# Attention on one Trainium2 core: P.V and row sum groups in two halves of 256 queries

## The chip, the cores and the metric

The kernel runs on one core of a Trainium2 chip. The metric is the device time of one execution in microseconds. Engines are named as in the profile: PE is TensorE, DVE is VectorE, ACT is ScalarE, POOL is GpSimd, SP is the engine that issues most loads and stores.

## The reference

The input is 8 batches of 2048 tokens with 256 features. A routed feed-forward block, self-attention and the same feed-forward block follow one another, each with a residual. The change touches attention alone, which is computed after the projections q, k, v for 8 heads of 32 features:

```python
scores = jnp.einsum('bqhd,bkhd->bhqk', q, k) / DH ** 0.5
attn = jax.nn.softmax(scores, axis=-1)
out = jnp.einsum('bhqk,bkhd->bqhd', attn, v)
```

## The kernel before, in words

The whole program is a row of phases, each with a barrier behind it: a scoring pass, the choice of tokens, the routed feed-forward block, the projections, attention (`attend`), and again scoring, choice and feed-forward. Everything is in fp32; scores use the fp32r form.

`attend` cuts the work into 64 units: 8 batches, 2 groups of four heads, 4 slices of 512 queries. A unit runs over 16 chunks of 128 keys, in 16 cycles. For one chunk and one head, a score tile is keys by queries, 128x512, in one of two PSUM banks (`ps_s`); ACT takes the exponential of each tile into `probs`, a ring of 8 chunks. There is no running maximum: the maximum of each query is computed a unit ahead by a second set of score matmuls (`ps_max`, queries by keys) which DVE reduces, and it enters the scores as an additional row of the operands. The order on each engine is written out by hand; semaphores join the engines.

A cycle `i` of a unit on PE, in the loop over `NCYC`:

- `score(j)` and `score(j + 1)`, heads 0 and 1 of chunk `i`. Each is one matmul (L1653) and waits until ACT has read the tile before the last (`exp_done`).
- `pv` of the chunk before (L1617): four matmuls, one for each head, each into its own 32 rows of `ps_acc`, 512 columns wide. fp32 makes each two passes, so the trace has eight records. For chunks 13 and 15 four more with a matrix of ones (L1625) add the same probabilities to the row sum in `ps_misc`. The last matmul increments `pv_done`.
- `score(j + 2)` and `score(j + 3)`, heads 2 and 3.
- `max_four` (L1584): four matmuls of 32 rows each, one per head, into the four banks of `ps_max`. They wait until DVE has reduced the four before.

Some cycles hold more. In cycle 0 the P.V group is that of chunk 15 of the unit before, and ACT copies the finished accumulator behind it (`copy_acc`, L1543). In cycle 3 `close_z` (L1633) adds POOL's part of the row sum, and ACT copies that (`copy_z`). In cycle 4 and cycle 6 four transposes each turn the row sum and the output (L1640, L1647). In cycle 13 the second score is put off: a transposition of the maxima (L1590) takes its bank, ACT copies it out, and then the score runs.

POOL sums the probabilities of the other chunks, so that PE need not (L1437, eight additions a unit, 128x2048 each). For five pairs of chunks a DMA adds the first into the second (L1414, 1 MB each); it is issued by POOL and waits until `pv_done` says that PE has read the second chunk of the pair. ACT may overwrite a chunk of the ring when PE, POOL and the DMA are done with it. The additions are issued in program order on POOL's queue, the waits for the pairs among them. `close_z` waits for the last addition.

Between the first score of a cycle and the last two, the order of the waits on PE is what sets its schedule:

```python
if i > 0:
    pv(unit, un, i - 1)
elif carry:
    pv(unit - 1, (un - 1) % BU, NC - 1)
...
for n in range(2, PER_CYC):
    pe.wait_ge(exp_done, unit * TILES + j + n - 1)
    score(j + n)
...
max_four(i)
```

`carry` is true for all units but the first.

## Time and profile before

| | us |
|---|---|
| median of 3 runs | 4966.07 |
| lowest, highest | 4965.32, 4968.26 |
| the profiled execution, its own time | 4967.85 |
| its span in the trace | 4965.8 |
| PE busy | 3964.8 |
| DVE busy | 3282.3 |
| ACT busy | 2837.2 |
| POOL busy | 2799.9 |

The span is the time from the first to the last record of the trace; the device time is a little longer. Busy times are unions of records. Four P.V matmuls run side by side in four column strips, so their records overlap, and the busy time of the group is far below the sum of the records. "PEld" are the weight loads of PE. In the timelines, records of one kind that follow one another are merged into one row ("x8"), with the time from the first start to the last end; in square brackets stands the idle time of the engine before the row, and what ended it.

### The profile page before, as it was taken

The page shows a single profiled execution, that of the slowest core. Times are in us where ns is not written, and L with a number is a line of the kernel's source. Part 1 is how long each engine was busy: PE and PEld are TensorE (multiplying, and loading weights), DVE is VectorE, ACT ScalarE, POOL GpSimd, SP SyncE. Part 2 cuts the span into 40 slices and gives each one's busy share as a digit, 9 for nine tenths or more (in the row PEclk, how much of TensorE's full clock was granted, in tenths as well). Part 3 has the DMA queues.
Part 4 walks back from the last instruction along what each step waited for, and adds up shares of the span by engine and source line. Part 5 has one row for each costly group of instructions (what it writes and reads, how often), then busy time and mean ns, then how long its engine had stood idle before and what let it go on. Part 6 is the DMA issues. An engine that isn't in the chain of part 4 may idle for free. (4 is left out here: it accounts for less than half of the span.)

```text
span 4965.8 us, 69030 instructions
## 1 busy us (share of the span) xinstructions
PE 3964.8 (80%) x21362; PEld 1556.9 (31%) x21362; DVE 3282.3 (66%) x3736; ACT 2837.2 (57%) x5622; POOL 2799.9 (56%) x966
## 2 busy tenths in 40 slices
PE   0156476599999999999999999999999999910266
PEld 0134354133333333333333333333333333300144
DVE  8744365677767767767776776777677777469644
ACT  4143355266666666666666666666666666623043
POOL 0011000377777877777787777778777777743111
PEclk9999788699999999999999999999999999955598
DMA  6200499557667665756756676675756764566200
GB/s 221 78 26 5 157 352 326 117 110 154 129 143 152 131 143 115 162 125 136 161 121 141 128 158 132 135 157 107 158 125 142 158 128 101 116 197 213 76 5 5
DMA packets 316558, 676.10 MB, mean 136 GB/s; under 512 B 24780, under 2 KB 208608, under 8 KB 268832
## 3 DMA queue, kind: packets, MB, share of 16 engines
q0 software_dynamic: 48000, 340.81, 33.8%
q1 hardware_dynamic: 234624, 297.04, 20.7%
q10 hardware_dynamic: 33568, 33.69, 2.0%
q8 instruction: 191, 3.13, 0.3%
q14 instruction: 175, 1.43, 0.1%
HBM read 198.90 MB, written 136.48 MB: 68 GB/s over the span
## 5 line engine op out<-in xcount | busy, mean ns | idle before, releaser
L1457 DVE TENSOR_REDUCE at_part_max<-at_ps_max 128x4 f32<-128x2048 f32 x1024 | 2348.4, 2293 | 1018.8 <-PE at_ps_max L1584 1017.7
L1556 ACT ACTIVATE at_probs<-at_ps_s 128x512 f32<-128x512 f32 x4096 | 2233.2, 596 | 1044.3 <-PE at_ps_s L1653 988.2
L1437 POOL TENSOR_TENSOR at_pool_sum<-at_pool_sum,at_probs 128x2048 f32<-128x2048 f32 x448 | 2056.5, 4590 | 283.7 <-DMA at_probs<-at_probs 271.0
L1653 PE MATMUL at_ps_s<-at_qs,at_ks 97*128 97x512 f32 (+1 forms) x4096 | 1715.3, 472 | 71.7 <-ACT at_probs L1556 36.3
L1653 PEld LDWEIGHTS at_ps_s<-at_qs,at_ks 97*128 97x128 f32 (+1 forms) x4096 | 682.4, 188 | 1496.0 <-ACT at_probs L1556 1201.0
L1617 PE MATMUL at_ps_acc<-at_probs,at_v 128*32 128x512 f32 x8192 | 1097.0, 608 | 0.9 <-ACT at_probs L1556 0.9
L1584 PE MATMUL at_ps_max<-at_ks,at_qs 32*128 32x512 f32 x4096 | 524.7, 501 | 87.7 <-DVE at_part_max L1457 43.3
L1414 POOL DMA_DIRECT2D at_probs<-at_probs x320 | 282.2, 882 | 498.9 <-PE at_ps_acc L1617 468.7
L1437 POOL TENSOR_TENSOR at_pool_sum<-at_probs 128x2048 f32<-128x2048 f32 x64 | 292.2, 4565 | 97.1 <-ACT at_probs L1556 97.1
L1584 PEld LDWEIGHTS at_ps_max<-at_ks,at_qs 32*128 32x128 f32 x4096 | 198.1, 183 | 442.1 <-DVE at_part_max L1457 296.4
L233 PE MATMUL s_pt<-s_ident,s_sall 128*128 128x128 f32 x2 | 0.9, 446 | 384.1 <-DVE s_sall L202 384.1
L1617 PEld LDWEIGHTS at_ps_acc<-at_probs,at_v 128*32 128x32 f32 x8192 | 161.4, 108 | 256.7 <-issue 247.7
L1394 POOL MEMSET at_ones<- 128x128 f32 x1 | 0.2, 204 | 336.8 <-POOLq L62 336.8
L1182 PE MATMUL pr_pqk<-pr_xT,pr_w 128*128 128x512 f32 x256 | 132.6, 666 | 36.5 <-DVE pr_lo L1085 33.4
L215 ACT ACTIVATE s_y<-s_x,s_small 128x256 f32<-128x256 f32 x256 | 129.2, 587 | 55.4 <-DVE s_small L198 55.4
L175 DVE CUSTOM_DVE_ANT_0 s_junk<-s_x,s_w 128x256 f32<-128x256 f32 x256 | 155.3, 607 | 0.0
L560 POOL TENSOR_TENSOR f_att<-f_att,f_rowsum 128x1280 f32<-128x1280 f32 x16 | 49.5, 3096 | 175.3 <-DVE f_rowsum L645 175.3
L154 POOL TENSOR_TENSOR s_x<-s_x,s_add 128x1024 f32<-128x1024 f32 x32 | 76.7, 2418 | 119.2 <-DMA s_add<-attention 119.2
L1625 PE MATMUL at_ps_misc<-at_probs,at_ones 128*32 128x512 f32 x1024 | 137.1, 607 | 0.0
L747 ACT ACTIVATE f_att<-f_att,f_rowmax 128x128 f32<-128x128 f32 x256 | 98.7, 388 | 45.5 <-DVE f_rowmax L641 45.5
L233 PEld LDWEIGHTS s_pt<-s_ident,s_sall 128*128 128x128 f32 x2 | 0.4, 180 | 384.5 <-issue 384.5
L1141 ACT ACTIVATE pr_hi<-pr_pqk,pr_bias 128x512 fp32r<-128x512 f32 x128 | 83.8, 683 | 60.1 <-PE pr_pqk L1182 59.8
(196 smaller groups left out, 2486.9 us busy)
## 6 DMA issues: line engine op xcount, KB each, us to landing
at_probs<-at_probs POOLq DMA_DIRECT2D x320, 1024.0 KB, 7.3
qk_parts<-pr_hi SPq DMA_DIRECT2D x32, 1024.0 KB, 6.4
qk_parts<-pr_lo SPq DMA_DIRECT2D x32, 1024.0 KB, 6.2
at_qs<-qk_parts SPq DMA_DIRECT2D x320, 64.0 KB, 1.9
at_ks<-qk_parts SPq DMA_DIRECT2D x80, 256.0 KB, 5.6
s_x<-in_x SPq DMA_DIRECT2D x16, 1024.0 KB, 7.6
after_ffn<-s_y ACTq DMA_DIRECT2D x16, 1024.0 KB, 8.4
pr_x<-after_ffn SPq DMA_DIRECT2D x8, 2048.0 KB, 12.4
```

The lines of the kernel that those rows point to most:

```text
L175: nc.vector.tensor_tensor_reduce(out=junk[:, t % 4, :], in0=xb[:, k, t, :], in1=w[:], scale=1.0, scalar=0.0, op0=ALU.mult, op1=ALU.add, ac ...
L215: last = nc.scalar.activation(yb[:, k, t, :], xb[:, k, t, :], ACT.Identity, scale=sm[:, k, 0, t:t + 1], bias=sm[:, k, 1, t:t + 1])
L747: last = nc.scalar.activation(att[:, s, h], att[:, s, h], ACT.Exp, scale=ATT_SCALE, bias=rowmax[:, s, h:h + 1], accum_out=rowsum[:, s, h:h ...
L1182: nc.tensor.matmul(pqk[:, m, :], w[:, m // NG, m % NG, :], xT[:, n % 2, m % NG, :], start=True, stop=True).then_inc(qk_done, 1)
L1414: nc.gpsimd.dma_start(probs[:, c % RING], probs[:, a % RING], accum_op=ALU.add).then_inc(dma_added[(un * ND + d) % 2], 16)
L1437: nc.gpsimd.tensor_tensor(acc, a, probs[:, c % RING], ALU.add).then_inc(pool_added, 1)
L1457: nc.vector.reduce_max(part_max[:, :, t, c], ps_max[:], AX.X).then_inc(part_max_done, 1)
L1556: nc.scalar.activation(probs[:, c % RING, h], ps_s[:, j % 2], ACT.Exp, scale=SCALE).then_inc(exp_done, 1)
L1584: last = nc.tensor.matmul(ps_max[:, h], qs[rows, un % NQB, h, t * P:(t + 1) * P], ks[rows, un % BU // NU, h, c * 512:(c + 1) * 512], start ...
L1617: last = nc.tensor.matmul(ps_acc[h * DH:(h + 1) * DH, :], v[:, k // NU, c, h * DH:(h + 1) * DH], probs[:, c % RING, h], start=(c == 0), st ...
L1625: last = nc.tensor.matmul(ps_misc[h * DH:(h + 1) * DH, :], ones[:, 0:DH], probs[:, c % RING, h], start=(c == RAW_CHUNKS[0]), stop=False)
L1653: nc.tensor.matmul(ps_s[:, j % 2], ks[rows, g, h, c * P:(c + 1) * P], qs[rows, un % NQB, h, :], start=True, stop=True).then_inc(scores, 1)
```

## The change

Each P.V group and each row sum group is cut into two halves of 256 queries. The first half stands between the second and the third score of a cycle, the second half behind the fourth. `max_four` moves from the end of the cycle to the place between the second score and the first half. Chunk 0 of a unit (cycle 1) is not cut: its whole group stands at the place of the second half. The ones matmuls of chunk 13 (cycle 14) are not cut either and stand there too. `pv_done` and `z_done` are incremented at the second half. ACT's copy of the accumulator moves from behind the second exponential of cycle 0 to behind the fourth.

```diff
--- before.py
+++ after.py
@@ -1555,7 +1555,7 @@
                         act.wait_ge(scores, unit * TILES + j + 1)
                         nc.scalar.activation(probs[:, c % RING, h], ps_s[:, j % 2], ACT.Exp, scale=SCALE
                                              ).then_inc(exp_done, 1)
-                        if carry and j == 1:
+                        if carry and j == PER_CYC - 1:
                             copy_acc(unit)
                         if carry and j == CLOSE_Z_IN * PER_CYC + 3:
                             copy_z(unit)
@@ -1608,31 +1608,46 @@
                     carry = un > 0 or not first_batch
                     g, u = un // NU, un % NU
 
-                    def pv(n, k, c):
-
-                        if c == 0 and carry:
-
-                            pe.wait_ge(oT_done, n)
+                    def pv_half(n, k, c, half):
+
+                        cols = slice(half * UQ // 2, (half + 1) * UQ // 2)
+                        if c == 0:
+                            if half == 0:
+                                return
+                            cols = slice(0, UQ)
+                            if carry:
+
+                                pe.wait_ge(oT_done, n)
                         for h in range(HG):
-                            last = nc.tensor.matmul(ps_acc[h * DH:(h + 1) * DH, :],
-                                                    v[:, k // NU, c, h * DH:(h + 1) * DH], probs[:, c % RING, h],
-                                                    start=(c == 0), stop=(c == NC - 1))
+                            last = nc.tensor.matmul(ps_acc[h * DH:(h + 1) * DH, cols],
+                                                    v[:, k // NU, c, h * DH:(h + 1) * DH], probs[:, c % RING, h, cols],
+                                                    start=(c == 0),
+                                                    stop=(c == NC - 1 and half == 1))
                         if c in RAW_CHUNKS:
-                            if c == RAW_CHUNKS[0] and carry:
-
-                                pe.wait_ge(o_done, n)
+                            first = c == RAW_CHUNKS[0]
+                            if first and half == 0:
+                                return
+                            if first:
+                                cols = slice(0, UQ)
+                                if carry:
+
+                                    pe.wait_ge(o_done, n)
                             for h in range(HG):
-                                last = nc.tensor.matmul(ps_misc[h * DH:(h + 1) * DH, :], ones[:, 0:DH],
-                                                        probs[:, c % RING, h], start=(c == RAW_CHUNKS[0]), stop=False)
-                        last.then_inc(pv_done, 1)
-
-                    def close_z(n, k):
-
-                        pe.wait_ge(pool_added, n * ADDS + ADDS)
+                                last = nc.tensor.matmul(ps_misc[h * DH:(h + 1) * DH, cols], ones[:, 0:DH],
+                                                        probs[:, c % RING, h, cols], start=first, stop=False)
+                        if half == 1:
+                            last.then_inc(pv_done, 1)
+
+                    def close_z(n, k, half):
+
+                        cols = slice(half * UQ // 2, (half + 1) * UQ // 2)
+                        if half == 0:
+                            pe.wait_ge(pool_added, n * ADDS + ADDS)
                         for h in range(HG):
-                            last = nc.tensor.matmul(ps_misc[h * DH:(h + 1) * DH, :], ones[:, 0:DH],
-                                                    pool_sum[:, k % 2, h], start=False, stop=True)
-                        last.then_inc(z_done, 1)
+                            last = nc.tensor.matmul(ps_misc[h * DH:(h + 1) * DH, cols], ones[:, 0:DH],
+                                                    pool_sum[:, k % 2, h, cols], start=False, stop=(half == 1))
+                        if half == 1:
+                            last.then_inc(z_done, 1)
 
                     def turn_z(n):
                         pe.wait_ge(zT_done, n)
@@ -1684,28 +1699,32 @@
                             if i == 0 and not carry:
                                 pe.wait_ge(max_row_done, 1)
                             score(j + 1)
-                        if i > 0:
-                            pv(unit, un, i - 1)
-                        elif carry:
-                            pv(unit - 1, (un - 1) % BU, NC - 1)
-                        if carry and i == CLOSE_Z_IN:
-                            close_z(unit - 1, un - 1)
-                        if turning:
-                            pe.wait_ge(max_row_done, unit + 2)
-                            score(j + 1)
-                        for n in range(2, PER_CYC):
-
-                            pe.wait_ge(exp_done, unit * TILES + j + n - 1)
-                            score(j + n)
-                        if carry and i == TURN_Z_IN:
-                            turn_z(unit)
-                        if carry and i == TURN_O_IN:
-                            turn_o(unit)
                         max_four(i)
+                        for half in range(2):
+                            if half == 1:
+                                if turning:
+                                    pe.wait_ge(max_row_done, unit + 2)
+                                    score(j + 1)
+                                for n in range(2, PER_CYC):
+
+                                    pe.wait_ge(exp_done, unit * TILES + j + n - 1)
+                                    score(j + n)
+                                if carry and i == TURN_Z_IN:
+                                    turn_z(unit)
+                                if carry and i == TURN_O_IN:
+                                    turn_o(unit)
+                            if i > 0:
+                                pv_half(unit, un, i - 1, half)
+                            elif carry:
+                                pv_half(unit - 1, (un - 1) % BU, NC - 1, half)
+                            if carry and i == CLOSE_Z_IN:
+                                close_z(unit - 1, un - 1, half)
                 if last:
                     pe.wait_ge(exp_done, (b * BU + BU) * TILES)
-                    pv(b * BU + BU - 1, BU - 1, NC - 1)
-                    close_z(b * BU + BU - 1, BU - 1)
+                    for half in range(2):
+                        pv_half(b * BU + BU - 1, BU - 1, NC - 1, half)
+                    for half in range(2):
+                        close_z(b * BU + BU - 1, BU - 1, half)
                     turn_z(b * BU + BU)
                     turn_o(b * BU + BU)
 
```

On PE, a regular cycle before (row maximum group, scores and P.V, from cycle 6 of a unit into cycle 7; the unit's names: `at_ps_s` scores, `at_ps_max` scores for the maximum, `at_ps_acc` P.V):

```order
L1584 MATMUL at_ps_max<-at_ks,at_qs 128x512 x4
L1653 MATMUL at_ps_s<-at_qs,at_ks 128x512 x2
L1617 MATMUL at_ps_acc<-at_probs,at_v 32x512 x4
L1653 MATMUL at_ps_s<-at_qs,at_ks 128x512 x2
L1584 MATMUL at_ps_max<-at_ks,at_qs 128x512 x4
```

The same place after the change:

```order
L1668 MATMUL at_ps_s<-at_qs,at_ks 128x512 x2
L1584 MATMUL at_ps_max<-at_ks,at_qs 128x512 x4
L1622 MATMUL at_ps_acc<-at_probs,at_v 32x256 x4
L1668 MATMUL at_ps_s<-at_qs,at_ks 128x512 x2
L1622 MATMUL at_ps_acc<-at_probs,at_v 32x256 x4
L1668 MATMUL at_ps_s<-at_qs,at_ks 128x512 x2
```

The P.V group of 512 columns has become two of 256, one on each side of a pair of scores, and the maximum group stands before the first of them.

On PE, cycles 13 and 14 of a unit before, from the score ahead of the turned maximum (L1590) to the ones group of chunk 13:

```order
L1653 MATMUL at_ps_s<-at_qs,at_ks 128x512
L1590 MATMUL at_ps_s<-at_ident,at_neg_max 16x128
L1617 MATMUL at_ps_acc<-at_probs,at_v 32x512 x4
L1653 MATMUL at_ps_s<-at_qs,at_ks 128x512 x3
L1584 MATMUL at_ps_max<-at_ks,at_qs 128x512 x4
L1653 MATMUL at_ps_s<-at_qs,at_ks 128x512 x2
L1617 MATMUL at_ps_acc<-at_probs,at_v 32x512 x4
L1625 MATMUL at_ps_misc<-at_probs,at_ones 32x512 x4
```

And after:

```order
L1668 MATMUL at_ps_s<-at_qs,at_ks 128x512
L1590 MATMUL at_ps_s<-at_ident,at_neg_max 16x128
L1584 MATMUL at_ps_max<-at_ks,at_qs 128x512 x4
L1622 MATMUL at_ps_acc<-at_probs,at_v 32x256 x4
L1668 MATMUL at_ps_s<-at_qs,at_ks 128x512 x3
L1622 MATMUL at_ps_acc<-at_probs,at_v 32x256 x4
L1668 MATMUL at_ps_s<-at_qs,at_ks 128x512 x2
L1584 MATMUL at_ps_max<-at_ks,at_qs 128x512 x4
L1622 MATMUL at_ps_acc<-at_probs,at_v 32x256 x4
L1668 MATMUL at_ps_s<-at_qs,at_ks 128x512 x2
L1622 MATMUL at_ps_acc<-at_probs,at_v 32x256 x4
L1636 MATMUL at_ps_misc<-at_probs,at_ones 32x512 x4
```

The maximum group of cycle 13 now stands behind the turned maximum and before the first half of chunk 12. The ones matmuls (L1625, now L1636) of chunk 13 keep their width and stand behind the second half.

## Rows read from the trace of the kernel before

**Rows 1.** Page, part 1: busy time and share of each engine.
```profile
PE 3964.8 (80%) x21362; PEld 1556.9 (31%) x21362; DVE 3282.3 (66%) x3736; ACT 2837.2 (57%) x5622; POOL 2799.9 (56%) x966
```

**Rows 2.** Windows, the stretch of attention: length, busy us (instructions), clock, DMA.
```profile
941.00:4357.00 3416.00, 3333.16 (x18387) 1154.45 (x18387) 2366.66 (x1194) 2293.45 (x4284) 2599.67 (x830) 0.99 0.64 135
```

**Rows 3.** Waits of the whole span: engine, line, releaser: us, times, longest.
```profile
PEld at_ps_s L1653 <- ACT at_probs L1556: 1201.0, 2421, 1.0
```

**Rows 4.** Timeline, PE weight loads, cycle 9: start, us, engine, line [idle before].
```profile
2520.57 0.19 PEld L1653 LDWEIGHTS at_ps_s<-at_qs,at_ks 97*128 97x128 f32 x1 [0.30 <-ACT at_probs L1556]
2521.00 0.16 PEld L1617 LDWEIGHTS at_ps_acc<-at_probs,at_v 128*32 128x32 f32 x8 [0.24 <-issue]
2521.99 0.30 PEld L1653 LDWEIGHTS at_ps_s<-at_qs,at_ks 97*128 97x128 f32 x2 [0.84 <-ACT at_probs L1556]
...
2523.66 0.19 PEld L1653 LDWEIGHTS at_ps_s<-at_qs,at_ks 97*128 97x128 f32 x1 [0.30 <-ACT at_probs L1556]
```

**Rows 5.** Page part 5, the exponentials; and the ACT timeline from cycle 9.
```profile
L1556 ACT ACTIVATE at_probs<-at_ps_s 128x512 f32<-128x512 f32 x4096 | 2233.2, 596 | 1044.3 <-PE at_ps_s L1653 988.2
...
2522.53 1.79 ACT L1556 ACTIVATE at_probs<-at_ps_s 128x512 f32<-128x512 f32 x3 [0.82 <-PE at_ps_s L1653]
```

**Rows 6.** Timeline, PE weight loads, cycle 6 with transposes, into cycle 7.
```profile
2512.59 0.30 PEld L1653 LDWEIGHTS at_ps_s<-at_qs,at_ks 97*128 97x128 f32 x2 [0.84 <-ACT at_probs L1556]
...
2513.70 0.19 PEld L1584 LDWEIGHTS at_ps_max<-at_ks,at_qs 32*128 32x128 f32 x4 [0.17 <-issue]
2514.13 0.32 PEld L1653 LDWEIGHTS at_ps_s<-at_qs,at_ks 97*128 97x128 f32 x2 [0.24 <-issue]
2514.80 0.16 PEld L1617 LDWEIGHTS at_ps_acc<-at_probs,at_v 128*32 128x32 f32 x8 [0.34 <-issue]
2515.80 0.30 PEld L1653 LDWEIGHTS at_ps_s<-at_qs,at_ks 97*128 97x128 f32 x2 [0.84 <-ACT at_probs L1556]
```

**Rows 7.** Timeline, PE weight loads, cycle 3 with the closing group.
```profile
2500.92 0.19 PEld L1653 LDWEIGHTS at_ps_s<-at_qs,at_ks 97*128 97x128 f32 x1 [0.30 <-ACT at_probs L1556]
2501.36 0.16 PEld L1617 LDWEIGHTS at_ps_acc<-at_probs,at_v 128*32 128x32 f32 x8 [0.25 <-issue]
2501.81 0.13 PEld L1633 LDWEIGHTS at_ps_misc<-at_pool_sum,at_ones 128*32 128x32 f32 x4 [0.30 <-POOL at_pool_sum L1437]
...
2503.21 0.30 PEld L1653 LDWEIGHTS at_ps_s<-at_qs,at_ks 97*128 97x128 f32 x2 [0.84 <-issue]
```

**Rows 8.** Timeline, PE weight loads, scores C of cycles 0, 1 and 2.
```profile
2492.97 0.30 PEld L1653 LDWEIGHTS at_ps_s<-at_qs,at_ks 97*128 97x128 f32 x2 [0.84 <-issue]
...
2496.15 0.30 PEld L1653 LDWEIGHTS at_ps_s<-at_qs,at_ks 97*128 97x128 f32 x2 [0.84 <-ACT at_probs L1556]
...
2499.25 0.30 PEld L1653 LDWEIGHTS at_ps_s<-at_qs,at_ks 97*128 97x128 f32 x2 [0.84 <-ACT at_probs L1556]
```

**Rows 9.** Timeline, PE weight loads: C of 12, D of 13, C of 14.
```profile
2531.28 0.30 PEld L1653 LDWEIGHTS at_ps_s<-at_qs,at_ks 97*128 97x128 f32 x2 [0.84 <-ACT at_probs L1556]
...
2535.34 0.19 PEld L1653 LDWEIGHTS at_ps_s<-at_qs,at_ks 128*128 128x128 f32 x1 [0.89 <-ACT at_probs L1556]
...
2538.81 0.30 PEld L1653 LDWEIGHTS at_ps_s<-at_qs,at_ks 97*128 97x128 f32 x2 [0.84 <-issue]
```

**Rows 10.** Timeline, PE weight loads, groups M of cycles 4 and 5.
```profile
2507.41 0.19 PEld L1584 LDWEIGHTS at_ps_max<-at_ks,at_qs 32*128 32x128 f32 x4 [0.17 <-issue]
...
2510.31 0.19 PEld L1584 LDWEIGHTS at_ps_max<-at_ks,at_qs 32*128 32x128 f32 x4 [0.52 <-DVE at_part_max L1457]
```

**Rows 11.** Timeline, POOL: last additions, a pair DMA, last additions of the next unit.
```profile
2492.25 9.21 POOL L1437 TENSOR_TENSOR at_pool_sum<-at_pool_sum,at_probs 128x2048 f32<-128x2048 f32 x2 [1.32 <-DMA at_probs<-at_probs]
...
2522.67 0.88 POOL L1414 DMA_DIRECT2D at_probs<-at_probs  x1
...
2542.62 9.21 POOL L1437 TENSOR_TENSOR at_pool_sum<-at_pool_sum,at_probs 128x2048 f32<-128x2048 f32 x2 [1.61 <-DMA at_probs<-at_probs]
```

**Rows 12.** Line 1414, the pair DMAs: time from issue to landing.
```profile
DMA to landing us min/median/max: 6.9/7.3/11.6
```

## The prediction

> **What bounds the kernel now.** I read the windows of the stretches first, then the waits, the chain and the timeline. The chain that ended last covers only the last feed-forward part and says nothing of the place of the change. The windows do: 3416 of 4965.8 us are attention, with PE busy 3333 of them at a granted clock of 0.99, that is 2.4 GHz, and DVE, ACT and POOL each under 80% [rows 1, 2]. A busy PE is not yet a bound. The waits show the weight loads of scores held 2421 times by ACT's exponentials, 1201 us in all [rows 3]: ACT and PE wait for each other in a ring, and the timeline shows it. I call the scores of a cycle A, B, C, D, the row-maximum group M and the P.V group PV. Times are starts of weight loads.
>
> An ordinary cycle [rows 4]: B at 2520.57, PV 0.43 later, C 0.99 (elsewhere 1.00) after that, the next B at 2523.66, 1.67 after C, held by ACT. ACT starts the exponential of C 0.54 after C's load, and one takes 0.60 [rows 5]; the 1.13 left hold that of C and of D, the second starting 0.5 behind the first. So the cycle is 0.43 + 0.99 + 1.67 = 3.09 us. D, M and A lie inside the 1.67 and cost nothing.
>
> The other PE prices: two scores without a wait, up to the next kind of group, 0.66 to 0.67, unrounded 0.66; M up to the next score 0.43; four transposes behind C and D make C to M 1.10 [rows 6]. A second group of four 512-column matmuls takes PV to C from 1.00 to 1.85, so 0.86 for the columns alone and 0.43 for 256 of them [rows 7]. A PV group of half width thus costs 1.00 - 0.43 = 0.57, not 0.50.
>
> **The change in a regular cycle.** The order becomes A B M half C D half. The leg from C to B holds D, the second half and A: 0.66 + 0.57 = 1.23 up to A, and A needs another 0.33, so B would be ready at 1.56. ACT still decides, at 1.67. The leg from B to C becomes 0.43 (B) + 0.43 (M) + 0.57 (half) = 1.43, where B and PV took 1.42. M has moved out of the hidden leg into the exposed one, and as much of P.V the other way. So +0.01 a cycle.
>
> A switch between kinds is in these prices. Two scores stream 1024 columns at 2.4 GHz in 0.43 of their 0.66; a load of 128 columns takes 0.11 (two loads 0.30, one 0.19), which leaves 0.12; B leaves 0.43 - 0.21 - 0.11 = 0.11, and so does M [rows 4, 6]. The change has five instead of four in a cycle. The fifth, from D to the second half, lies in the hidden leg. The one from M to a half is new: M works in four strips of 32 rows, PV in four strips of 32 columns, and so far scores always stood between them. I take 0.11 like its neighbours, because it is a switch from M as the one in [rows 6] is; its bounds are 0 (both are strips) and 0.22 (out and back in). The Trainium skill, page TensorEngine Tiling (Array Packing), section Key Properties, says that a change of tiling mode drains TensorE. By that rule five drains for four speak against the change. The rows agree that a switch costs time, but set the fifth where ACT hides it.
>
> **The change in the other cycles**, C to C. A unit is 52.9 us (45.84 from its first C to the fifteenth, then 3.10 and 3.96) [rows 7, 8, 9]:
> - Into cycle 0 (P.V and row sum of chunk 15) and into cycle 3 (closing of the row sum), before 3.96 each. Now 1.67 + 0.43 + 0.43 + 1.00 (two half groups) = 3.53: -0.43 twice.
> - Cycle 0 to 1, before 3.18 [rows 8]. ACT's copy of the accumulator moves behind the exponential of D and waits for the second halves: it starts about 1.75 after C, the next exponential 0.5 later, and that ends at 2.85; C follows at 2.90: -0.28. Cycle 1 has no first half, its whole P.V stands behind D, and D waits for the late exponential of B, about 0.49 after C: 0.49 + 0.44 + 1.00 + 0.66 + 0.43 + 0.57 = 3.59 for 3.10: +0.49.
> - Cycle 3 to 4: the second halves of P.V and of the closing no longer fit beside ACT: 0.66 + 1.00 + 0.66 + 0.43 + 0.57 = 3.32 for 3.10: +0.22. Cycles 4 and 6, with transposes: 1.10 + 0.57 + 0.66 + 0.43 + 0.57 = 3.33 for 3.18 and 3.21: +0.27 in all.
> - Cycle 12 to 14, before 7.53 [rows 9]: up to the score D of cycle 13 (4.06) nothing changes, since M and a half stand where PV stood. Then 0.43 + 0.57 + 0.66 + 0.43 + 0.57 = 2.66: 6.72, so -0.81. The whole ones group of chunk 13 now follows the second half of cycle 14: 0.66 + 0.57 + 0.86 + 0.66 + 0.43 + 0.57 = 3.75 for 3.10: +0.65.
> - Six regular cycles: +0.06.
>
> Sum: -0.86 - 0.28 + 0.49 + 0.22 + 0.27 - 0.81 + 0.65 + 0.06 = -0.26 a unit, a difference of sixteen rounded terms. 63 units carry work over: -16 us.
>
> DVE stays out of it. Its M to M minimum is 2.90 [rows 10], under the new intervals but one, where it costs some hundredths. POOL does not stay out. Each of its five paired DMAs a unit waits for the P.V of a chunk, which is signalled at B + 1.42 now and at B + 0.43 + 0.43 + 0.57 + 0.66 + 0.57 = B + 2.66 then, 1.24 later. Behind that wait stand POOL's later additions, and the closing group of cycle 3 waits for the last of them. In the unit shown they end at 2501.46, 0.35 before the closing group loads; in the next at 2551.83, some 3 us before it [rows 7, 11]. Of all 64 pairs, the first and the last included, 13 are closer than 1.24, and their shortfalls sum to 10 us; with units 0.26 shorter besides, to about 13. So +13.
>
> PE also issues more: 68 more matmuls a unit, in two passes each, 8704 more records. Their loads run under the passes before, and what shows of them is in the 0.57. No cost of their own.
>
> Net -16 + 13 = -3 us. The profiled execution took 4967.85 (span 4965.8), so 4965 for its like; it lies 1.8 above the median of the three runs shown, so the forecast in their terms is **4963 us**. About 0.2% (10 us) is what a measurement can tell from no change, so this is "the same".
>
> **Rivals.**
> *The switch from M to a half is cheaper.* At 0.06 instead of 0.11 the exposed leg is 0.05 shorter in 15 of 16 cycles: 15 x 0.05 x 63 = -47 us, of which POOL's lateness, larger in a shorter unit, takes about 6: 4922. For it: both groups use strips. Against: the switches seen cost the same whatever their kinds. Here I also count milder luck, the irregular cycles gaining and landings short: 4950. Chance 0.31.
> *The switch is dearer*, which ends slower. It stands on the exposed leg just behind M. At 0.16 it is +47, less 4 that POOL gives back: 5006; at 0.22 5060. It decides from about 0.125 on. The same place of the ring would suffer if the second half did not fit in the hidden leg: all 0.11 of a fifth switch in 1008 cycles is +111, 5074; against that stand the 0.11 of room. That is also where the page's drain rule, named above, would lead. Chance 0.17.
> *POOL becomes the bound.* Its own loop, from one last addition to the next, is 50.4 us beside a unit of 52.9 [rows 11], with landings of 7.3 us in the median and up to 11.6 [rows 12]. Pairs started 1.24 later meet other loads. If each landing takes 0.5 more, the four behind one another cost 2.0, and with the 1.24 that exceeds the room in more than half of the units: about 0.7 a unit, +45, 5008. Chance 0.15.
> *As forecast*, within 10 us of 4966: 0.37.
>
> **How the numbers follow.** Faster 0.31, same 0.37, slower 0.17 + 0.15 = 0.32. The range takes in a switch of 0.06 at one end and one of 0.16 or a late POOL at the other: 4924 to 5010. The far ends of the unseen switch, 0 and 0.22, stay outside with about 2 in 10.
>
> **What would show it.** Right: some 30,000 PE matmul records; B to C 1.43 and C to B 1.67 in cycles 8 to 12, a period of 3.09 to 3.11; M to the first half 0.43; half to C 0.57; 3.5 into cycles 0 and 3, 3.75 into cycle 15; pair DMAs about 1.2 later against B; POOL holding the closing group in about 13 more units. Wrong: a regular period off 3.10 by over 0.03 (the switch), B later than 1.67 after C (the hidden leg overflows), or the closing group waiting for POOL in most units.

## The result, and the profile after

| | before | after |
|---|---|---|
| median, us | 4966.41 (5 runs) | 4992.05 (5 runs) |
| profiled execution, its span | 4967.85, 4965.8 | 4994.06, 4992.0 |
| attention, first score to last C | 3414.5 | 3438.5 |
| a unit's 16 intervals C to C, medians summed | 52.92 | 52.81 |
| closing groups that follow POOL's last addition within 0.2 us | 5 of 64 | 25 of 64 |
| pair DMAs, issue to landing, median | 7.3 | 7.6 |

The ratio is 1.0053, with the 95% interval [1.0039, 1.0067]: the change makes the kernel 26 us slower, where "the same" (4963) was forecast. The time lies in the range, the direction is that of one of the rivals. Single intervals and counts in this part come from the starts in the trace; unit numbers count from 0, eight to a batch.

The page of the kernel after, part 1 and the P.V group of part 5; compare [rows 1]:

```profile
PE 3994.0 (80%) x30066; PEld 1727.0 (35%) x30066; DVE 3279.8 (66%) x3736; ACT 2844.4 (57%) x5622; POOL 2806.5 (56%) x966
...
L1622 PE MATMUL at_ps_acc<-at_probs,at_v 128*32 128x256 f32 (+1 forms) x15872 | 1302.4, 400 | 0.1
```

The 30066 records are the expected 8704 more. PE is 29 us busier, ACT and POOL are 7 us busier each.

The timeline of PE's weight loads, a regular cycle of the kernel after, B to B:

```profile
2532.73 0.19 PEld L1668 LDWEIGHTS at_ps_s<-at_qs,at_ks 97*128 97x128 f32 x1 [0.25 <-ACT at_probs L1556]
2533.16 0.19 PEld L1584 LDWEIGHTS at_ps_max<-at_ks,at_qs 32*128 32x128 f32 x4 [0.25 <-DVE at_part_max L1457]
2533.60 0.16 PEld L1622 LDWEIGHTS at_ps_acc<-at_probs,at_v 128*32 128x32 f32 x8 [0.25 <-issue]
2534.17 0.30 PEld L1668 LDWEIGHTS at_ps_s<-at_qs,at_ks 97*128 97x128 f32 x2 [0.41 <-ACT at_probs L1556]
2534.83 0.16 PEld L1622 LDWEIGHTS at_ps_acc<-at_probs,at_v 128*32 128x32 f32 x8 [0.37 <-issue]
2535.40 0.19 PEld L1668 LDWEIGHTS at_ps_s<-at_qs,at_ks 97*128 97x128 f32 x1 [0.41 <-ACT at_probs L1556]
2535.84 0.19 PEld L1668 LDWEIGHTS at_ps_s<-at_qs,at_ks 97*128 97x128 f32 x1 [0.25 <-ACT at_probs L1556]
```

B to M is 0.43, M to the first half 0.44, the half to C 0.57, C to the next B 1.67: 3.11 for the 3.09 of [rows 4]. The second half, the row at 2534.83, takes 0.57 as well, and the next A follows at 2535.40, 1.23 after C as worked out; B still waits for ACT. The unseen switch, from M to a half, costs what the others cost. The same timeline at D of cycle 13, C of cycle 14 and C of cycle 15:

```profile
2488.71 0.19 PEld L1668 LDWEIGHTS at_ps_s<-at_qs,at_ks 128*128 128x128 f32 x1 [0.89 <-ACT at_probs L1556]
...
2491.36 0.30 PEld L1668 LDWEIGHTS at_ps_s<-at_qs,at_ks 97*128 97x128 f32 x2 [0.41 <-ACT at_probs L1556]
...
2495.13 0.30 PEld L1668 LDWEIGHTS at_ps_s<-at_qs,at_ks 97*128 97x128 f32 x2 [0.41 <-ACT at_probs L1556]
```

From D to C of cycle 14 it takes 2.65 (2.66 forecast, 3.47 in [rows 9]), and to the next C 3.77 (3.75). So PE's schedule came out as worked out, and a little in favour of the change. What did not is the closing group of cycle 3. Waits of its weight loads for POOL, in us, times and longest, before and after; the longest is that of the very last closing, behind the last unit:

```profile
PEld at_ps_misc L1633 <- POOL at_pool_sum L1437: 11.9, 7, 7.2
```

```profile
PEld at_ps_misc L1647 <- POOL at_pool_sum L1437: 39.2, 21, 11.6
```

One such place, POOL at the end of unit 28 (compare [rows 11]):

```profile
2492.89 0.87 POOL L1414 DMA_DIRECT2D at_probs<-at_probs  x1
2493.49 4.87 POOL L1437 TENSOR_TENSOR at_pool_sum<-at_pool_sum,at_probs 128x2048 f32<-128x2048 f32 x1
2502.50 9.16 POOL L1437 TENSOR_TENSOR at_pool_sum<-at_pool_sum,at_probs 128x2048 f32<-128x2048 f32 x2 [4.13 <-DMA at_probs<-at_probs]
```

and PE there, first half, closing half, scores, second half:

```profile
2507.74 0.16 PEld L1622 LDWEIGHTS at_ps_acc<-at_probs,at_v 128*32 128x32 f32 x8 [0.24 <-issue]
2511.72 0.20 PEld L1647 LDWEIGHTS at_ps_misc<-at_pool_sum,at_ones 128*32 128x32 f32 x8 [3.82 <-POOL at_pool_sum L1437]
2512.73 0.50 PEld L1668 LDWEIGHTS at_ps_s<-at_qs,at_ks 97*128 97x128 f32 x2 [0.81 <-issue]
2513.88 0.20 PEld L1622 LDWEIGHTS at_ps_acc<-at_probs,at_v 128*32 128x32 f32 x8 [0.65 <-issue]
```

The last pair's DMA is issued at 2492.89 and its addition starts at 2502.50, 9.6 later. The two last additions end at 2511.66, and PE, which was ready some 0.5 after 2507.74, closes at 2511.72. The windows before, in and after this wait (length, then PE, PEld, DVE, ACT, POOL busy, granted clock, DMA share, GB/s):

```profile
2496.50:2507.30 10.80, 10.69 (x82) 4.06 (x82) 7.36 (x4) 7.59 (x15) 6.59 (x3) 1.00 0.49 123
2507.30:2511.70 4.40, 1.08 (x13) 0.35 (x12) 2.29 (x1) 0.76 (x2) 4.40 (x2) 0.88 0.00 0
2511.70:2517.00 5.30, 5.28 (x32) 1.90 (x32) 0.00 (x0) 2.09 (x4) 5.22 (x2) 0.50 0.01 3
2517.00:2522.70 5.70, 5.70 (x50) 2.41 (x50) 4.11 (x3) 3.51 (x8) 3.79 (x1) 0.96 0.00 0
```

Then comes the second cost: behind that wait of 3.82 us the granted clock is 0.50, that is 1.2 GHz, and with two passes of closing matmuls, the scores and P.V at half speed PE is busy all the time until 2517 with what usually takes half of it. Unit 29, in whose cycle 3 this closing stands, takes 58.9 us; the median is 52.9. The Trainium skill's page TensorE: Matmul & The Clock Gate (section HAM oscillation — how this bites in real kernels) says that a wait of TensorE between bursts of matmuls, if it is long enough, makes the next burst start at the lower clock; the trace agrees for this wait. The shorter waits went either way: one of 2.09 us in unit 9 came with the lower clock and its unit is 6.1 us too long, while one of 2.31 us in unit 9 of the kernel before left the clock at 1.00 and cost 1.6.

The sum for the profiled pair, from unit lengths against their median: the shorter units give -7; lengthening outside the loop edges between batches goes from about 1.5 to about 30, in ten units, of which units 9, 29, 45 and 57, those with a fallen clock, hold 24; the five loop edges give +3. That is the +24 of attention. In the four units PE's waits are 2.09, 3.82, 4.38 and 2.26, together 12.5, so by my estimate the other half of their 24 is the lower clock. Behind the last C the final closing adds 4.8 (15.2 to 20.0), and the stages outside attention take 2 to 3 less.

### The profile page after: what moved, and what is told of

It is laid out like the page before. It is cut to its first block and busy times, and to the rows that moved or that the text cites. A ratio compares the mean times of both kernels' runs of the same rounds, so it can differ in the third digit from the quotient of the medians.

```text
span 4992.0 us, 86438 instructions
## 1 busy us (share of the span) xinstructions
PE 3994.0 (80%) x30066; PEld 1727.0 (35%) x30066; DVE 3279.8 (66%) x3736; ACT 2844.4 (57%) x5622; POOL 2806.5 (56%) x966
## 3 DMA queue, kind: packets, MB, share of 16 engines
q14 instruction: 176, 1.43, 0.1%
## 5 line engine op out<-in xcount | busy, mean ns | idle before, releaser
L1668 PE MATMUL at_ps_s<-at_qs,at_ks 97*128 97x512 f32 (+1 forms) x4096 | 1653.2, 467 | 56.3 <-ACT at_probs L1556 29.5
L1622 PE MATMUL at_ps_acc<-at_probs,at_v 128*32 128x256 f32 (+1 forms) x15872 | 1302.4, 400 | 0.1
L1668 PEld LDWEIGHTS at_ps_s<-at_qs,at_ks 97*128 97x128 f32 (+1 forms) x4096 | 667.5, 188 | 1135.9 <-ACT at_probs L1556 989.9
L1622 PEld LDWEIGHTS at_ps_acc<-at_probs,at_v 128*32 128x32 f32 x15872 | 313.0, 108 | 574.3 <-issue 573.4
L1636 PE MATMUL at_ps_misc<-at_probs,at_ones 128*32 128x256 f32 (+1 forms) x1536 | 147.8, 457 | 0.0
```

The source lines that it names most:

```text
L1622: last = nc.tensor.matmul(ps_acc[h * DH:(h + 1) * DH, cols], v[:, k // NU, c, h * DH:(h + 1) * DH], probs[:, c % RING, h, cols], start=(c ...
L1636: last = nc.tensor.matmul(ps_misc[h * DH:(h + 1) * DH, cols], ones[:, 0:DH], probs[:, c % RING, h, cols], start=first, stop=False)
L1668: nc.tensor.matmul(ps_s[:, j % 2], ks[rows, g, h, c * P:(c + 1) * P], qs[rows, un % NQB, h, :], start=True, stop=True).then_inc(scores, 1)
```

## The experiments

**POOL's last addition taken away, on both kernels.** POOL leaves out chunk 14, so its chain is 4.6 us shorter, and the row sum lacks that chunk.

```diff
-    pool_chunks = [c for c in range(NC) if c not in RAW_CHUNKS and c not in dma_sources]
+    pool_chunks = [c for c in range(NC) if c not in RAW_CHUNKS and c not in dma_sources and c != 14]
```

On the kernel after: 

> The kernel after, but POOL leaves out its addition of chunk 14 (the row sum lacks that chunk). Theory L (late signal): in the kernel after, the P.V signal for the pair DMAs comes 1.24 us later against the scores, POOL's last addition arrives late at the closing group in 25 units, and PE waits there and then runs at the lower clock; the PE schedule itself is about 0.12 us a unit shorter. Then POOL's chain, 4.6 us shorter here, is never late: no closing group waits, units of 52.8, time about 4957, 7 to 9 below its partner with the old order. Rival S (schedule): the split order itself costs the 26 us (a fifth switch, an exposed maximum group), POOL's waits are a by-product: the time stays within 5 of 4992.

On the kernel before: 

> The kernel before, POOL leaves out chunk 14 in the same way (row sum lacks it). Both theories: it loses only the few closing waits of the kernel before (5 units), so 4962 to 4965, units of 52.91. Partner of the run without chunk 14 on the kernel after: theory L puts this one 7 to 9 us above it, rival S some 25 us below it.

Measured 4959.0 (ratio 0.9990 [0.998, 1.000]) and 4959.3 (0.9986 [0.9977, 0.9995]). Without late closings the two orders are the same; the profiled pair has attention 6.0 us shorter with the new order, the medians do not show it, and the second run lies below what I expected of it. The 26 us between the two orders are gone, so they go through POOL's chain, and rival S falls.

**A late signal on the old order.**

```diff
                         pool.wait_ge(pv_done, unit * NC + c + 1)
+                        pool.wait_ge(exp_done, unit * TILES + (c + 1) * HG + 3)
```

> The kernel before with its PE order untouched; POOL's issue of each pair DMA waits in addition for the exponential of the third score (C) of the same cycle, which ends about 1.1 us after the P.V signal. Theory L: lateness alone does it: pair DMAs 1.1 us later, closing groups waiting in 15 to 25 units, +12 to +30 us (4978 to 4996). Rival S: within 5 us of the kernel before.

4980.1 (1.0029 [1.0017, 1.0040]), inside the expected span. I took it for a proof; the trace says otherwise: 8 closings follow POOL within 0.2 us, not 15 to 25, and most of the 14 us lie elsewhere, see below at the last pair.

**The last two additions exchanged, on the kernel after.** Everything is computed.

```diff
-    pool_chunks = [c for c in range(NC) if c not in RAW_CHUNKS and c not in dma_sources]
+    pool_chunks = [c for c in range(NC) if c not in RAW_CHUNKS and c not in dma_sources and c != 12] + [12]
```

> The kernel after with POOL's last two additions exchanged (chunk 14, which needs no DMA, before chunk 12, which waits for the last pair); everything is computed. Theory L: the addition of 14 fills the wait for the last landing, the chain ends up to 4 us earlier in late units, closing waits fall from 25 to a few, time 4957 to 4964, so below the kernel before. Rival S: 4985 or more.

4961.8, ratio 1.0000 [0.9991, 1.0009]: 30 us below the kernel after, level with the one before. The waits of the closing group for POOL, in us, times and longest:

```profile
PEld at_ps_misc L1647 <- POOL at_pool_sum L1437: 10.3, 2, 10.0
```

10.3 us are left of 39.2, nearly all in the final closing. The pair DMAs still land after 7.6 us in the median, as they do in the kernel after and in the run without chunk 14; so the longer landings do not come from the late closings. The exchange alone, on the kernel before:

> The kernel before with POOL's last two additions exchanged, PE's order untouched. Theory: the kernel before had 5 late closing groups, worth 2 to 5 us beside those of the start of a batch; with the exchange 4961 to 4965, no closing wait but the very last. It tells what the exchange is worth by itself (little), against 30 us in the kernel after. If the exchange helped for another reason than the closing wait, it would help here as much.

4965.6 (0.9999 [0.9990, 1.0008]). So the exchange is worth 30 us with the new order and nothing with the old one.

**The exposed leg.** The maximum group moved between B and a whole P.V, on the kernel before:

```diff
                             score(j + 1)
+                        max_four(i)
                         if i > 0:
                             pv(unit, un, i - 1)
...
-                        max_four(i)
```

> The kernel before with only the maximum group moved, to the place between score B and the whole P.V. Ring theory (the exposed leg from B to C adds to the 1.67 that ACT needs from C to B): leg B to C 0.43 + 0.43 + 1.00 = 1.86, a period of 3.53 in regular cycles, some 7 us a unit, about 5410 us. Rival (PE is bound by the sum of its groups and the number of switches, which is the same four as before): the period stays at 3.10 and the time within 10 of 4966.

5396.4 (1.0867 [1.0847, 1.0887]). The timeline, B, M, P.V, C, B, with the transposes of cycle 6 behind C:

```profile
2544.68 0.19 PEld L1653 LDWEIGHTS at_ps_s<-at_qs,at_ks 97*128 97x128 f32 x1 [0.30 <-ACT at_probs L1556]
2545.11 0.19 PEld L1584 LDWEIGHTS at_ps_max<-at_ks,at_qs 32*128 32x128 f32 x4 [0.25 <-issue]
2545.55 0.16 PEld L1617 LDWEIGHTS at_ps_acc<-at_probs,at_v 128*32 128x32 f32 x8 [0.24 <-issue]
2546.54 0.30 PEld L1653 LDWEIGHTS at_ps_s<-at_qs,at_ks 97*128 97x128 f32 x2 [0.84 <-ACT at_probs L1556]
...
2548.22 0.19 PEld L1653 LDWEIGHTS at_ps_s<-at_qs,at_ks 97*128 97x128 f32 x1 [0.30 <-ACT at_probs L1556]
```

0.43 + 0.44 + 0.99 + 1.68 = 3.54, where PE's sum and the switches are as before. The ring is what bounds.

**Halves with the maximum group at the end of the cycle**, that is `max_four(i)` of the kernel after moved behind the loop over the halves:

> The kernel after with the maximum group moved back to the end of the cycle, behind the second half: A B half C D half M. Ring theory with a second ring (from A through its and B's exponential to D 1.67, from D back to A the groups that stand there: 0.44 + 0.57 + 0.43 = 1.44): the period stays at 3.09 to 3.11, since the maximum group only changes the leg; with cycles 1, 5, 7 and 13 some tenths longer a unit of 53.6, so 5005 to 5030 with POOL's waits. Rival (only the leg B to C counts, now 1.00): PE's sum of 2.90 bounds, 12 us less in regular cycles per... in all about 4850. Rival of the switch count (five, as in the kernel after): unchanged, 4992.

5058.1 (1.0190 [1.0174, 1.0205]), above the expected 5005 to 5030: period 3.11, units of 54.06. A and B, D, and the next A and B:

```profile
2526.21 0.30 PEld L1668 LDWEIGHTS at_ps_s<-at_qs,at_ks 97*128 97x128 f32 x2 [0.24 <-issue]
...
2527.88 0.19 PEld L1668 LDWEIGHTS at_ps_s<-at_qs,at_ks 128*128 128x128 f32 x1 [0.25 <-ACT at_probs L1556]
...
2529.32 0.30 PEld L1668 LDWEIGHTS at_ps_s<-at_qs,at_ks 97*128 97x128 f32 x2 [0.24 <-ACT at_probs L1556]
```

From A to D it takes 1.67, from D to the next A 1.44. The second ring exists: D waits for B's exponential just as B waits for D's. The irregular cycles took 0.5 a unit more than my sum for them; cycle 15, 0.20 longer than in the kernel after, was not in it.

**Both legs made equal.** Both rings have 1.67 of ACT in them, so the groups outside, together 2.44 with five switches, should be shared evenly. A cut at 384 queries gives 0.43 + 0.78 on one side and 0.44 + 0.36 + 0.43 on the other.

```diff
+    CUT = 384
...
-                        cols = slice(half * UQ // 2, (half + 1) * UQ // 2)
+                        cols = slice(half * CUT, CUT + half * (UQ - CUT))
```

with the maximum group last, and chunk 0 whole at the first place.

> Cut at 384 queries instead of 256, the maximum group behind the second piece, chunk 0 whole at the first place: legs B to C 0.43 + 0.78 = 1.21 and D to A 0.44 + 0.36 + 0.43 = 1.23. Ring theory: both rings at 2.90, which is also DVE's minimum, so regular periods of 2.90 and units of 50.6 to 50.8; POOL's own loop of 50.4 then bounds many units: 4865 to 4910 us. Rival (switches decide): like the kernel after, 4980 or more.

> The same with POOL's last two additions exchanged. Ring theory: units near 50.7 with fewer closing waits, 4840 to 4880 us, clearly below the kernel before and below the run without the exchange. If POOL's loop is the new bound whatever its order, no better than that run.

The first ran in 4992.4 (1.0057 [1.0042, 1.0073]), a miss, and by its time the rival's: but its regular period is 2.91 as forecast, its 16 intervals sum to 51.87, but 53 of 64 closings wait for POOL and PE spends 163 us of attention at the lower clock (40 in the kernel before, 68 in the kernel after). I had priced the waits and not the clock. With the additions exchanged: **4876.3**, ratio 0.9819 [0.9805, 0.9832]. Timeline of a cycle of that run, C, second piece, M, A and B, first piece, C:

```profile
2526.57 0.42 PEld L1669 LDWEIGHTS at_ps_s<-at_qs,at_ks 97*128 97x128 f32 x2 [0.62 <-ACT at_probs L1557]
2527.23 0.16 PEld L1623 LDWEIGHTS at_ps_acc<-at_probs,at_v 128*32 128x32 f32 x8 [0.24 <-issue]
2527.60 0.19 PEld L1585 LDWEIGHTS at_ps_max<-at_ks,at_qs 32*128 32x128 f32 x4 [0.21 <-DVE at_part_max L1458]
2528.03 0.40 PEld L1669 LDWEIGHTS at_ps_s<-at_qs,at_ks 97*128 97x128 f32 x2 [0.24 <-issue]
2528.70 0.16 PEld L1623 LDWEIGHTS at_ps_acc<-at_probs,at_v 128*32 128x32 f32 x8 [0.26 <-issue]
2529.48 0.41 PEld L1669 LDWEIGHTS at_ps_s<-at_qs,at_ks 97*128 97x128 f32 x2 [0.63 <-ACT at_probs L1557]
```

0.66 + 0.37 + 0.43 + 0.67 + 0.78 = 2.91: PE never waits long here, and this is DVE's 2.90 of [rows 10] as well.

**Whether the last pair is what comes late.** In the kernel after, the largest room between POOL's last addition and the closing group, leaving out the loop edges, is 1.30; before it was 3.60. That is a shift of 2.3, not 1.24, and the median room falls as much, from 2.75 to 0.48. 1.9 of it is a later issue: from the last pair's issue to the closing group it takes 17.6 instead of 19.5 in the median. The rest is POOL's way from that issue to its last addition's end, 17.0 for 16.6. The last pair waits for chunk 12, whose P.V stands in cycle 13, and there D's wait for ACT, 0.89 in the row at 2488.71 above, now lies ahead of the second half.

```diff
                         pool.wait_ge(pv_done, unit * NC + c + 1)
+                        pool.wait_ge(exp_done, unit * TILES + (c + 1) * HG + (4 if d == ND - 1 else 3))
```

> The kernel before, PE order untouched; pairs 0 to 3 wait for the exponential of score C of the same cycle (about 1.1 us later), the last pair (chunk 12, cycle 13) for that of score D, which is put off in that cycle: about 1.8 later in the median, 2.3 from the P.V signal, as the traces show it for the kernel after. Theory T (turning cycle): the last pair's lateness of 2.3 is what my sum missed; the largest room ahead of the closing group falls from 3.6 to about 1.3, and +22 to +32 us, 4988 to 4998. Rival U (lateness of 1.24 for all, the rest of the loss lies in the PE order): as the run with all pairs 1.1 late, 4980 +- 3.

The same with the last pair alone:

> The kernel before, only the last pair waits for the exponential of score D of cycle 13; the other four are as before. Theory T: most of the loss hangs on the last pair, since its landing and two additions (7.1 + 9.2) alone fill the way to the closing group: 4980 to 4994, the largest room 1.3. Rival U: the first pair delays all that follow, the last alone does little: 4966 to 4972.

4979.9 (1.0029 [1.0018, 1.0041]) and 4980.6 (1.0031 [1.0019, 1.0043]). The largest room is 1.39 and 1.38, as expected, closings wait in 13 and 12 units. But the first of the two, meant to repeat the lateness of the kernel after, missed its 4988 to 4998 and came out where rival U had it. The median room there is 1.01 and 1.09, not 0.48; from the last pair's issue to the closing group it takes 17.7, as in the kernel after, so the issue is as late; what it lacks is the longer landings (median 7.4, not 7.6). And the cost is elsewhere: outside the loop edges these runs lose 2.2 and 3.4 us (7.2 with all pairs 1.1 late), against 8 and 10 more than before at the five edges. PE at the edge from unit 15 to 16, in the kernel before and with the last pair late:

```profile
1791.19 0.19 PEld L1584 LDWEIGHTS at_ps_max<-at_ks,at_qs 32*128 32x128 f32 x4 [0.37 <-DVE at_part_max L1457]
1795.13 0.50 PEld L1653 LDWEIGHTS at_ps_s<-at_qs,at_ks 97*128 97x128 f32 x2 [3.75 <-issue]
```

```profile
1793.67 0.19 PEld L1586 LDWEIGHTS at_ps_max<-at_ks,at_qs 32*128 32x128 f32 x4 [0.37 <-DVE at_part_max L1459]
1799.29 0.50 PEld L1655 LDWEIGHTS at_ps_s<-at_qs,at_ks 97*128 97x128 f32 x2 [5.43 <-issue]
```

3.9 us from the last group of a batch to the first of the next became 5.6. DMA queues in the 1.6 us behind that last group, last pair late (q0 is the pair DMA):

```profile
q0 software_dynamic: 32, 0.13, 43.0%
q8 instruction: 2, 0.03, 13.2%
```

and in the kernel before, from the start of its first instruction packets:

```profile
q8 instruction: 2, 0.03, 5.7%
...
q0 software_dynamic: 1, 0.00, 0.0%
```

With the pair late, instruction packets start a microsecond after PE's last group has begun, at 1794.7, while the pair's packets still take 43% of the DMA engines' time. In the kernel before they started as the pair's last packet went, at 1790.7, 0.45 before that group. So they start 1.5 later against the group, and the gap is 1.7 longer. That the refetch of the loop waits behind the pair is my reading of these rows, and no run takes the pair away from an edge. The kernel after speaks against it in part: the pair's last packet goes 1.3 to 1.4 us behind PE's last load at four of its five edges, and the gaps there are 4.2 to 4.5. What the control can tell is whether the added instruction or the lateness does it:

> Control for the three runs with late pairs: the kernel before with a wait of the same form ahead of each pair DMA, but for an exponential that is always long done, so that nothing is later. In the traces of the three runs, some 10 of their 14 us lie at the five loop edges between batches (PE gap 3.8 to 4.3 us before, 5.6 to 6.6 there), not at closing groups. If that is the added instruction and not the lateness: about 4976, edge gaps near 6, no late closing groups. If the lateness makes the edges longer: 4963 to 4968.

4968.0 (1.0003 [0.9994, 1.0012]), edge gaps 3.9 to 4.4. It is the lateness and not the added instruction.

**Chunk 12 whole at the first place, on the kernel after.**

```diff
+                        if c == 12:
+                            if half == 1:
+                                return
+                            cols = slice(0, UQ)
...
-                        if half == 1:
+                        if half == 1 or c == 12:
                             last.then_inc(pv_done, 1)
```

> The kernel after with one group put back: the P.V of chunk 12 (cycle 13) stays whole, ahead of the put-off score B, so its signal comes before D's wait as in the kernel before. All other groups are halves. Theory T: the largest room is back to about 3.3, closing waits fall from 25 to about 12, cycle 12 to 14 no longer than now: 4965 to 4977. Rival U: within 5 of 4992.

5036.6 (1.0137 [1.0121, 1.0152]), a clear miss, though the signal is early (largest room 4.4, nine late closings). PE in cycles 13 and 14, P.V, B and C, D, A, B, M:

```profile
1606.72 0.16 PEld L1626 LDWEIGHTS at_ps_acc<-at_probs,at_v 128*32 128x32 f32 x8 [0.25 <-issue]
1607.71 0.30 PEld L1672 LDWEIGHTS at_ps_s<-at_qs,at_ks 97*128 97x128 f32 x2 [0.84 <-ACT at_max_row L1518]
1608.90 0.19 PEld L1672 LDWEIGHTS at_ps_s<-at_qs,at_ks 128*128 128x128 f32 x1 [0.89 <-ACT at_probs L1556]
1609.39 0.19 PEld L1672 LDWEIGHTS at_ps_s<-at_qs,at_ks 97*128 97x128 f32 x1 [0.30 <-ACT at_probs L1556]
1610.08 0.19 PEld L1672 LDWEIGHTS at_ps_s<-at_qs,at_ks 97*128 97x128 f32 x1 [0.51 <-ACT at_probs L1556]
1610.51 0.19 PEld L1584 LDWEIGHTS at_ps_max<-at_ks,at_qs 32*128 32x128 f32 x4 [0.24 <-issue]
```

```profile
1607.50:1610.90 3.40, 2.76 (x13) 1.05 (x9) 1.63 (x1) 2.46 (x5) 1.98 (x2) 1.00 0.93 185
1610.90:1614.30 3.40, 3.40 (x26) 1.30 (x26) 2.29 (x1) 1.40 (x3) 3.30 (x1) 0.50 1.01 205
1614.30:1620.00 5.70, 5.70 (x53) 2.08 (x46) 2.86 (x2) 3.26 (x6) 4.40 (x2) 1.00 0.22 55
```

From 1607.71 on PE has scores alone, with waits between them, since M and P.V have both gone ahead; and then the clock is 0.50 in cycle 14. It was so in some 30 units. The profiled execution is the slowest of the six, 5066.7. The run says nothing on the signal.

**Closing in cycle 4, and the loads of keys and values in another unit, on the kernel after.** The first sets `CLOSE_Z_IN`, `TURN_Z_IN`, `TURN_O_IN` to 4, 5, 7, the second changes `un == NU` to `un == NU + 1` ahead of `load_kv(b + 1, 0)`.

> The kernel after with the closing of the row sum in cycle 4 instead of 3 (its transposes in 5 and 7), everything computed. Theory L: the closing groups have 3.5 us more room, so no more than a few wait and PE's clock does not fall there: 4955 to 4963, below the kernel before. If something other than the closing wait costs the 26 us, 4985 or more.

> The kernel after, with the load of the next batch's keys and values in the sixth unit of a batch instead of the fifth. In the trace of the kernel after all expensive late closings but those of a batch's start belong to the fifth unit (of eight), whose first two pairs land after 9 to 11 us beside these loads. If the loads make those units late: the late closings move by one unit, the total stays near 4992. If they do not matter: the late ones stay where they are.

4980.6 (1.0030 [1.0019, 1.0042]), spread from 4971.5 to 4997.7, between the two forecasts. Closings wait in 4 units, the loss outside the edges falls from about 30 to about 3; but the edges cost 8 us more than before (first gap 6.7), the part behind the last C 7.6 more, and attention begins 5 later, for which I have no reason. So the closing wait in the middle is removed, and a late last pair finds other places.

With the loads moved 4985.1 (1.0042 [1.0027, 1.0058]). The long units after a fifth unit (29, 37, 45, 53) are gone, 30, 38, 46 and 54 have come, by 3.3 us in unit 30 and 0.4 in the others; 13 and 57 stay, and are longer. The loads make those units tight.

**The finding on the fast version.** Cut at 384, additions exchanged, closing in cycle 4:

> The version cut at 384 queries with the exchanged additions, and the closing in cycle 4. Its trace had 29 closing waits, 35 us in all. With the closing a cycle later most of them go: 4840 to 4860. If POOL's own loop bounds the unit, moving the closing only moves the wait: 4870 to 4880.

**4855.7**, ratio 0.9776 [0.9763, 0.9790]: 110 us below the kernel before, 136 below the kernel after. One closing waits, the final one.

## Why the prediction was wrong, point by point

- **The ring and the PE prices: right.** B to C 1.44 for 1.43, C to B 1.67, half 0.57, switch as its neighbours. Moving the maximum group alone cost 0.44 a cycle, its price.
- **The other cycles: right in all signs, 0.15 a unit too good.** Medians 3.54, 2.95, 3.59, 3.34, 3.34, 3.34, 6.75, 3.77 for 3.53, 2.90, 3.59, 3.32, 3.33, 3.33, 6.72, 3.75. The sum was -0.11 for -0.26: -7 us for -16.
- **"So +13" for POOL: the step that failed.** In the profiled pair it is 28 at the closing groups, 5 behind the last C and 3 at the edges, 36 in all. Three things were wrong in it. The first is the shift: I took 1.24 from a regular cycle for all pairs, while the last pair's signal stands in the cycle with D's wait: its issue comes 1.9 nearer to the closing group, and with the longer landings the room shrinks by 2.3; the same comparison of all 64 with 2.3 gives 19 units and 27 us. The second is that I gave a wait its own length as price: in four units the clock fell beside the wait, and they lost 24 for 12.5 of waiting. The third is that I kept the landings as they were: the median went from 7.3 to 7.6, and in the fifth units of a batch the third pair landed after 8.4 to 8.6 instead of 6.9, and the last after 7.9 to 9.7 instead of 7.3 to 8.3 (units 12, 20, 28, 44). The first alone does not make the loss: put on the old order, where the landings stayed at 7.3 to 7.4, it cost 2 to 3 us outside the edges. That the rest hangs on the landings is an inference from this difference; no run changed them alone, and why they are longer in the new order stays open.
- **The rival "POOL becomes the bound" comes nearest**; I gave it 0.15 and 5008. Its mechanism, longer landings on top of a later start, is what the fifth units show, with 0.3 in the median instead of its 0.5. But closing groups wait in 25 of 64 units, not in more than half, and half of what the four worst units lose is the clock, which the rival did not have. So POOL made single units late and did not set the pace of all.
- **The rival of the dearer switch and that of the cheaper one fell**: 0.44 where 0.43 was taken.
- **"No cost of their own" for the 8704 records: nothing speaks against it.** With POOL relieved both orders take the same time.

## What to carry to other kernels

When a group is cut or moved, follow the semaphore that its last instruction raises, pair by pair and in the very cycle in which each waiter needs it; the one in the irregular cycle may move farther, here 1.9 for 1.24. In a ring of two engines count what stands on each leg between one wait and the next: a group moved from a hidden leg to an exposed one eats the gain of the one that left, and the best cut is the one that makes the legs equal, here 384 and 128. And a late producer should do first what needs no transfer: exchanging two additions was worth nothing before, and 30 to 116 us in the orders with less room.

## What the runs showed of the hardware that I had not expected

- A wait of 3.82 us on PE made its unit 6.1 us longer than the median, with the granted clock at 0.50 afterwards. The length of the wait alone does not tell: beside one of 2.09 us the clock fell, behind one of 2.31 us it did not. It also fell in cycle 14 of some 30 units of one run where no wait was longer than 0.9 us, behind a stretch of scores alone with short waits between them.
- With a 1 MB DMA still under way when a loop jumped back, the gap on PE was 5.6 to 6.6 us instead of 3.8 to 4.3, and instruction packets started between the transfer's own. That the one holds up the other is not shown, and at four edges of the kernel after the gap was 4.2 to 4.5 with the transfer under way too.
- Passes of 128 columns in four strips cost no more than their share: that piece took 0.36 or 0.37, the 384 columns 0.78, together what two halves take, 1.14.
